# Attention B in 64x64 blocks, with its row maxima added by the mask product

## The reference

```
A_mem  = sigma(q) M / (sigma(q) . z + eps)              sigma(x) = elu(x) + 1
scores = q k^T / sqrt(8), -inf above the diagonal       (64 x 64)
A_dot  = softmax(scores) v
out    = beta A_mem + (1 - beta) A_dot
V_prev = sigma(k) M / (sigma(k) . z + eps)
M      = M + sigma(k)^T (v - V_prev);   z = z + sum(sigma(k))
```

## Time and profile before

| | |
|---|---|
| median of 3 runs | 2139.34 us (2138.98 to 2144.91) |
| the profiled execution's own time | 2121.74 us |
| its span | 2120.0 us |
| mean granted clock of TensorE | 0.854 |
| PE busy | 1713.4 us (81%) |
| DVE busy | 1494.4 us (70%) |
| ACT, POOL busy | 764.9 us (36%), 842.8 us (40%) |
| DMA | 159.66 MB, mean 75 GB/s |

### The profile page before, as it was taken

One profiled execution on the slowest core, in us unless ns is written; L12 is line 12 of the kernel. 1 busy time (PEld: TensorE's weight loads), 2 busy tenths in 40 slices (PEclk: granted clock), 3 DMA queues, 4 the chain that ended last, 5 costly groups with the idle time before them and its releaser, 6 DMA issues. The chain is left out here.

```text
span 2120.0 us, 45990 instructions
## 1 busy us (share of the span) xinstructions
PE 1713.4 (81%) x13668; PEld 1420.0 (67%) x13668; DVE 1494.4 (70%) x3615; ACT 764.9 (36%) x1663; POOL 842.8 (40%) x1054
## 2 busy tenths in 40 slices
PE   5999999999999999947665577787787887787787
PEld 3888888888888888845554355565565665665665
DVE  5678888888888888848885556665666666656655
ACT  1455555555555555522222122222222222222222
POOL 3445544455444455436564423232322232223331
PEclk8999999999999999968886677877887777777868
DMA  3322222222122222123331222222222222212221
GB/s 115 115 93 78 72 72 73 71 71 71 68 73 71 73 73 74 61 66 99 90 97 44 77 66 67 82 75 75 71 72 72 80 75 76 69 66 79 81 70 41
DMA packets 181309, 159.66 MB, mean 75 GB/s; under 512 B 10417, under 2 KB 162609, under 8 KB 181234
## 3 DMA queue, kind: packets, MB, share of 16 engines
q1 hardware_dynamic: 178930, 157.95, 22.6%
q10 hardware_dynamic: 2304, 0.79, 0.2%
HBM read 113.87 MB, written 44.83 MB: 75 GB/s over the span
## 5 line engine op out<-in xcount | busy, mean ns | idle before, releaser
L600 PE MATMUL a_bank<-a_vp,a_prob 128*128 128x96 f32 x4096 | 546.4, 278 | 0.3 <-ACT a_prob L457 0.3
L600 PEld LDWEIGHTS a_bank<-a_vp,a_prob 128*128 128x128 f32 x4096 | 512.8, 197 | 16.8 <-ACT a_prob L457 8.6
L633 DVE TENSOR_REDUCE a_nmax<-a_bank 128x2 f32<-128x512 f32 x512 | 331.7, 686 | 119.2 <-PE a_bank L527 118.8
L457 ACT ACTIVATE a_prob<-a_bank 128x512 f32<-128x512 f32 x512 | 306.0, 598 | 179.3 <-PE a_bank L582 170.5
L1429 ACT ACTIVATE c_prob<-c_bank 128x256 f32<-128x256 f32 x256 | 98.8, 386 | 353.0 <-PE c_bank L1510 317.9
L1707 DVE TENSOR_REDUCE c_nmax<-c_bank 128x4 f32<-128x512 f32 x256 | 168.8, 686 | 69.2 <-PE c_bank L1530 68.7
L527 PE MATMUL a_bank<-a_k_st,a_q_st 96*128 96x256 bf16 x1024 | 208.2, 286 | 7.7 <-DVE a_nmax L633 5.0
L1560 PE MATMUL c_o_bank<-c_vb,c_prob 128*128 128x96 f32 x1024 | 209.1, 339 | 2.3 <-DVE c_ad L1832 1.3
L582 PE MATMUL a_bank<-a_q_st,a_k_st 120*128 120x256 bf16 x1024 | 202.8, 280 | 0.0
L1506 PE MATMUL c_bank<-c_causal_t,c_ident 128*128 128x256 bf16 x256 | 84.9, 332 | 120.6 <-DMA c_q_st<-scratch_c_m_dram 113.8
L1560 PEld LDWEIGHTS c_o_bank<-c_vb,c_prob 128*128 128x128 f32 x1024 | 172.2, 239 | 10.1 <-ACT c_prob L1429 3.0
(11 more groups left out here) (195 smaller groups left out, 3141.6 us busy)
## 6 DMA issues: line engine op xcount, KB each, us to landing
a_q_st<-scratch_a_parts_dram SPq DMA_DIRECT2D x192, 96.0 KB
a_k_st<-scratch_a_parts_dram SPq DMA_DIRECT2D x64, 288.0 KB
c_q_st<-scratch_c_parts_dram SPq DMA_DIRECT2D x192, 96.0 KB
c_k_st<-scratch_c_parts_dram SPq DMA_DIRECT2D x64, 288.0 KB
scratch_a_parts_dram<-a_parts SPq DMA_DIRECT2D x32, 384.0 KB, 2.7
scratch_c_parts_dram<-c_parts SPq DMA_DIRECT2D x32, 384.0 KB, 3.0
a_x<-in_x SPq DMA_DIRECT2D x32, 128.0 KB, 10.7
scratch_y<-a_y SPq DMA_DIRECT2D x32, 128.0 KB, 9.4
```

The costliest lines, as they stand in the source:

```text
L457: act.activation(prob[h % 4][:, :, :].rearrange("p a b -> p (a b)"), t_ps[h % 2][:, :], ACT.Exp).then_inc(exped, 1)
L600: mm = pe.matmul(o_ps[g % 2][:, at:at + VC], prob[h % 4][:, c, t * P:(t + 1) * P], vp[o][:, c, :], start=c == 0, stop=c == NT - 1)
L633: dve.tensor_reduce(nmax[:, t, 2 * g:2 * g + 2], s_ps[t][:, :].rearrange("p (h k) -> p h k", h=2), AX.X, ALU.max, negate=True).then_inc(ma ...
```

## The change

- **First pass.** A unit is now eight heads by two segments: `causal` holds the 64x64 mask eight times, and 16 products of 64 columns each write a 64x64 diagonal block, segment 2t to the lower and segment 2t+1 to the upper 64 partitions. There are four units a batch (NU = 4), one in each of slots 1, 2, 4 and 5, and DVE reduces four times instead of eight.
- **Maxima.** ACT's copy writes the transposed parts into rows 64 to 87 of `late[h2]`, whose rows 0 to 63 hold the causal mask. The second pass's first product has `late` as its moving operand and `pick` as its weights (identity rows for the mask, and for each g rows that pick the three parts of its two heads); it writes mask and maxima at once. The write to DRAM, `shift_rows` and the ones in `k_st` are gone. SP issues `stack(1)` right behind `stack(0)`.
- **Contraction.** Products of both passes contract all 128 rows of the stacks; rows 72 to 127 are zero.
- **Order.** L1541's transposes move behind the transposes of `at` in slot 0, and ACT's `skn` copy to the start of slot 1. On PE, `mem` 0 stands behind slot 1's unit and ahead of the values; `read` 0 ahead of slot 2's unit, `read` 1 behind slot 4's unit, `read` 2 in slot 7. On DVE, `remember` and `read` stand ahead of the slot's reduction, `remember(2)` is interleaved with the second split in slot 6, and `read(2)` is in slot 7.
- **Semaphores.** `stack_in` is now four, one for each buffer and half.

```diff
+        BROWS = SEG + NPART * H // 2
-        causal, causal_t = sb("causal", [P, 512], BF16), sb("causal_t", [P, T], BF16)
+        causal = sb("causal", [P, 512], BF16)
+        pick, late = sb("pick", [BROWS, H // 4, 2, SEG], BF16), two("late", [BROWS, T], BF16)
...
-        mt_ps = ps_a[0:NPART * H // 2, 0:T // 2].bitcast(BF16)
+        mt_ps = ps_a[SEG:BROWS, 0:T // 2].bitcast(BF16)
...
                     stack(0)
-                if active(j, u, 1):
-                    shift_rows(0)
-                    shift_rows(1)
-                if active(j, u, 0):
                     stack(1)
...
-                            act.copy(mt[h2][:, :], mt_ps).then_inc(mt_d, 1)
-                            act.wait_ge(mt_d, 2 * b + h2 + 1)
-                            if h2 or later(j, b, 1):
-                                act.wait_ge(mt_out, (2 * b + h2) * 16)
-                            act.dma_start(m_dram[1 - i, h2], mt[h2][:, :]).then_inc(mt_out, 16)
+                            act.copy(late[h2][SEG:BROWS, :], mt_ps).then_inc(mt_d, 1)
...
                         if g % (ST // 2) == 0:
-                            pe.wait_ge(m_in[g // (ST // 2)], (b + 1) * 16)
+                            pe.wait_ge(mt_d, 2 * b + g // (ST // 2) + 1)
...
-                        pe.matmul(t_ps, ident16[:, :], causal_t[:, :], start=True, stop=True)
+                        pe.matmul(t_ps, pick[:, g % (ST // 2), :, :].rearrange("p a k -> p (a k)"),
+                                  late[g // (ST // 2)][:, :], start=True, stop=True)
...
-                                               k_st[st][0:KROWS, 2 * g + hh, cs], q_st[st][0:KROWS, 2 * g + hh, cs],
+                                               k_st[st][:, 2 * g + hh, cs], q_st[st][:, 2 * g + hh, cs],
...
+                    if s in (2, 7) and active(j, u, 1):
+                        recalled(s // 3)
                     if s in S_AT and active(j, u, 1):
...
+                        pe.matmul(s_ps[t][:, :], ident16[:, :], causal[:, :], start=True, stop=True)
+                        for c in range(H // 2):
+                            for p in range(2):
+                                ts = slice((2 * t + p) * SEG, (2 * t + p + 1) * SEG)
+                                mm = pe.matmul(s_ps[t][p * SEG:(p + 1) * SEG, c * SEG:(c + 1) * SEG],
+                                               q_st[o][:, h2 * H // 2 + c, ts], k_st[o][:, h2 * H // 2 + c, ts],
+                                               start=False, stop=True, skip_group_check=True)
+                        mm.then_inc(score, 1)
+                    if s == 1 and active(j, u, 1):
+                        remembered(0)
+                    if s == 4 and active(j, u, 1):
+                        recalled(1)
...
+                    if s in (3, 5) and active(j, u, 1):
+                        remembered(s // 2)
...
+                    if s == 1 and active(j, u, 1):
+                        for k in range(2):
+                            remember(0, k)
+                    if s == 2 and active(j, u, 1):
+                        for k in range(4):
+                            read(0, k)
+                    if s == 4 and active(j, u, 1):
+                        for k in range(2):
+                            remember(1, k)
+                        for k in range(4):
+                            read(1, k)
                     if s in S_AT and active(j, u, 1):
-                        for t in range(NT):
-                            reduce_unit(S_AT.index(s), t)
+                        reduce_unit(S_AT.index(s))
```

More of the change, by code:

```diff
@@ L1422, in body @@
                 for s in range(ST):
+                    if s == 1 and active(j, u, 1):
+                        b = n - 1
+                        act.wait_ge(sk_p, b + 1)
+                        if later(j, b, 1):
+                            act.wait_ge(mem_p, b * 3)
+                        act.copy(skn[0:SEG, :, :].rearrange("p s f -> p (s f)"),
+                                 ps_c[0:SEG, 0:(NS - 1) * P]).then_inc(sk_d, 1)
                     lag, g = turn(s)
@@ L1494, in body, with remembered, recalled @@
                 o = 1 - i
+                def remembered(c):
+                    b = n - 1
+                    if c == 0:
+                        pe.wait_ge(sk_d, b + 1)
+                        pe.wait_ge(vs_d, 2 * b + 1)
+                    else:
+                        pe.wait_ge(u_d, b * 2 + c)
+                    pe.matmul(ps_c[:, 0:MW], skn[:, c, :], uv[o][:, c, :], start=True, stop=True
+                              ).then_inc(mem_p, 1)
+                def recalled(c):
+                    b = n - 1
+                    pe.wait_ge(mz_d, b * 5 + 2 * c + 1)
+                    pe.matmul(ps_c[:, 0:MW], sg[o][:, c + 1, :, :].rearrange("p a t -> p (a t)"), mz[:, :],
+                              start=True, stop=True).then_inc(read_p, 1)
                 for s in range(ST):
@@ L1534, in body @@
-                    if s == 0 and active(j, u, 1):
-                        b = n - 1
-                        pe.wait_ge(sg_d, b + 1)
-                        if later(j, b, 1):
-                            pe.wait_ge(read_d, b * 9)
-                        apart(pe, spare)
-                        for c in range(NS - 1):
-                            mm = pe.transpose(ps_c[0:SEG, c * P:(c + 1) * P], sg[o][:, c, 0, :], ident[:, :])
-                        mm.then_inc(sk_p, 1)
+                            pe.wait_ge(mask_d, 6)
@@ L1573, in body @@
                         mm.then_inc(at_p, 1)
+                    if s == 0 and active(j, u, 1):
+                        b = n - 1
+                        pe.wait_ge(sg_d, b + 1)
+                        if later(j, b, 1):
+                            pe.wait_ge(read_d, b * 9)
+                        apart(pe, spare)
+                        for c in range(NS - 1):
+                            mm = pe.transpose(ps_c[0:SEG, c * P:(c + 1) * P], sg[o][:, c, 0, :], ident[:, :])
+                        mm.then_inc(sk_p, 1)
                     if s == 5 and active(j, u, 3):
```

137 lines of the change are left out of this document (52 added, 85 removed).

## The result

Faster, but not by as much as forecast: 2044.91 us (median of 4 runs, 2036.56 to 2053.96) against 2139.44 us of the kernel before, a ratio of 0.9553 [0.9496, 0.9611]. The forecast was 1949 us with a range of 1890 to 2010, so the time lies 35 us outside it. The profiled execution took 2052.87 us, with a span of 2050.7.

The account below looks back on a forecast made before the run. Waits and the clock, no full engine, were taken to bound attention B. Per batch 29.0 - 3.8 - 0.5 - 1.3 + 1.6 - 2.1 = 22.9 us, together 190 us saved, giving 1949 us; range 1890 to 2010.

Parts of the forecast that it names:

- maxima in the mask product: Slot 7, second pass: PE's wait for the maxima from DRAM goes, 3.8 us a batch less.
- four units: First pass: four units of 64-column products replace eight units, saving PE 0.5 us a batch.
- other moves of the memory chain: Memory-chain moves other than `read(0)` in slot 2, such as `recalled(2)` and the `sg` transposes: priced at 0.
- the -1.3 for `uv`: Slot 3: `read(0)` ahead of slot 2's reduction on DVE brings `uv` sooner, L1630 1.3 us earlier; bounds 0.7 and 1.7.
- Memory chain in other slots: Moving the memory chain to new slots saves 1.3 us a batch through `read(0)` in slot 2; other moves 0.
- The clock: Low-clock stretches behind the stalls of slots 3 and 7: half regained, 2.1 us a batch; bounds 0 and 4.3.
- 25.0 with none: The batch period in us if none of the lost clock came back, against 22.9 forecast.
- The waits late next: Slot 0: new PE waits for z and `ad`, 0.5 and 1.1 us, together 1.6 a batch; bounds 0.5 and 2.6.
- The unit: First pass: one mask and sixteen 64-column products take 0.77 us at full clock; over 1.2 would refute the forecast.
- rival C: First pass: 64-column products don't stream, 222 ns each; period 35.3 us, time 2328 us; chance 0.03.
- The ring: Path through DRAM from unit 0 to the next unit 0: 21.0 to 23.0 us a batch, nearly binds.
- Rival B: Ring and low clock feed each other through a wait for `stack(0)` before unit 0: 24.8 us, 2007 us; chance 0.22.

Follow-up runs that it names:

- e7: The kernel before with only the maxima added by the mask product (eight units, old slots, 96 rows in the first pass): 1970.86 us.
- e14: The changed kernel with the memory chain in its old slots and 96 instead of 128 contracted rows in both passes: 1949.64 us.
- e6: The changed kernel with the memory chain back in its old slots on PE, DVE and ACT: 1945.92 us.
- after: The changed kernel itself, with every part of the change, against the kernel before: 2044.91 us, ratio 0.9553.
- e13: The changed kernel with only DVE's `remember(1)` moved from slot 4 to the end of slot 3: 1958.88 us.
- e4: The changed kernel with DVE's `normed(1)` moved behind `remember(1)` and `read(1)` in slot 4: 1956.87 us.
- e9: The changed kernel with six unread 512-column products in slot 4 alone, ahead of PE's wait for `mz`: 1969.34 us.
- e11: The changed kernel with the memory chain in its old slots and the stack read by twelve DMAs a half instead of four: 1835.97 us.
- e15: The changed kernel, new slots kept, with the stack read by twelve DMAs a half instead of four: 2041.08 us.
- e1: The changed kernel with ten unread 512-column products a batch put ahead of PE's waits: 1905.22 us.
- e5: The kernel before with unread 512-column products in PE's two stalls, 14 in slot 7 and 6 in slot 3: 2118.35 us.
- e10: The changed kernel with the memory chain in its old slots and unread products in slots 0, 1 and 3 (4, 6 and 3): 1888.20 us.
- e3: The changed kernel with 96 instead of 128 contracted rows in both passes: 2100.32 us.
- e12: The changed kernel with old memory-chain slots, twelve stack DMAs a half, `late` and `pick` padded to 128 rows, and unread products in slots 0 and 3: 1837.52 us.

## Why the prediction was wrong, step by step

The runs cut the period into the prediction's own terms, 29.00 → 24.06 (e7) → 22.87 (e14) → 22.95 (e6) → 26.64 (after):

| step | forecast | measured |
|---|---|---|
| maxima in the mask product, waits for z and `ad`, clock | -3.8 + 1.6 - 2.1 = -4.3 | -4.9 |
| four units, with the wait for `uv` | -0.5 - 1.3 = -1.8 | -1.2 |
| 128 contracted rows | 0 | +0.1 |
| other moves of the memory chain | 0 | **+3.7** |
| sum | -6.1 | -2.4 |

The split holds for this order of the steps. e14 and e6 wait 1.6 and 2.2 us a batch for the stack, so the second and third steps may be worth more than the table gives where the ring is shorter, and the last one costs more. In the prediction the -1.3 for `uv` stood with the memory chain; it is placed here with the units, for the reason given below.

**The step that failed** is "Memory chain in other slots". It followed `read(0)` through slot 2 with care and then said "the other moves I price at 0". Two of them were weighed against the trace, that of `recalled(2)` and that of the `sg` transposes; `remember(1)` was not. On DVE it left slot 3, where its product is ready, and stands behind `normed(1)`, which waits for POOL's `rs`, while on PE `read` 1 moved ahead of the values of slot 4. What is queued behind a waiting instruction was to be named for this pair as well. In its place the runs showed a new wait of PE for `mz`, 1.4 us a batch, and a low clock behind it. e6 undoes the whole step (3.7 us), e13 moves this pair alone (3.3), and e4 leaves the pair and moves `normed(1)` behind it (3.3): both are within 0.01 us of each other. e13 keeps PE's new place, so DVE's place carries the cost; whether PE's old place alone would have covered it wasn't tried.

**The clock** was treated as a bonus with bounds of 0 and 4.3 us. It has another side: the step with a new wait of 1.4 us cost 3.7, of which e9 shows 2.8 to be the clock. Where that wait was missing, the clock rose (0.85 in e7, 0.89 in e6) and the term came in: e7's PE is busy 593.39 us where the kernel before has 676.55 for the same columns, 2.9 us a batch for the 2.1 priced. So the clock term was right for the kernel forecast and wrong for the one that ran; and the bound "25.0 with none" still didn't hold the result, because it kept 1.6 us of waits and had no room for a new one. Why the clock is granted as it is, from which activity, these runs don't settle.

**The -1.3 us for `uv`** came in, but for another reason: e7 has the old slots and keeps the wait, e6 has the old slots and four units and has lost it. So does e14, with 96 rows (4.9 us in 29 batches), which leaves the four units, with one reduction less in the slot; the new place of `read(0)` wasn't needed.

**Right:** the maxima's wait and its 3.8 us, the first part of the change and by itself most of the gain (e7, 1970.86 us). The waits late next: z 0.3 us (7.9/29) and `ad` 1.1 (33.3/29) for 0.5 and 1.1. Reductions, four a batch:

```profile
L1711 DVE TENSOR_REDUCE c_nmax<-c_bank 128x8 f32<-128x512 f32 x116 | 77.8, 679 | 9.4 <-PE c_bank L1533 9.1
```

The unit: the mask's load at 1577.48, sixteen loads in 0.33 us from 1577.91, the values' load at 1578.28, 0.8 us in all against 0.77 (PE, full clock):

```profile
1577.48 0.10 PEld L1529 LDWEIGHTS c_bank<-c_causal,c_ident 128*128 128x128 bf16 x1
1577.91 0.33 PEld L1533 LDWEIGHTS c_bank<-c_k_st,c_q_st 128*64 128x64 bf16 x16 [0.33 <-issue]
1578.28 0.52 PEld L1558 LDWEIGHTS c_o_bank<-c_vb,c_prob 128*128 128x128 f32 x4
```

That is 21 ns a load, so rival C is out. By the rule of the Trainium skill (TensorE: Matmul & The Clock Gate, LDWEIGHTS) a load of 64 columns would take 53 ns, an estimate worked out from its P/1.2 ns; the trace doesn't agree, and the measurement decides. The ring, forecast at 21.0 to 23.0 us, is where e6 stops (22.95, of them 2.2 waiting for the stack), and with the stack read by twelve DMAs the same work takes 19.58 (e11). In `after` it didn't bind (1.5 us of waits in all, and e15). Rival B, the nearest to the result at 2007, had a part of the mechanism, a wait with a low clock behind it, at the wrong wait; that the two feed each other, as B has it, these runs don't show.

**The tail** wasn't in the forecast at all. It is 7.9 us longer, with the clock at 0.53; with fill it is 41.3 us at 0.88 (e1). Which wait begins its low clock wasn't tried.

Of the signs that the prediction named, three showed the failure: PE's largest wait (L1493 instead of the stack's), the clock (0.76 where 0.8 to 0.95 was named) and the traffic (79 GB/s where over 90 was), which follows from the period.

## What to carry to other kernels

When a change reorders instructions, walk through every moved instruction on every engine and ask what now stands ahead of it and what that waits for; an "otherwise 0" must be earned as each priced term is. Price a new wait on TensorE at more than its length, since the clock behind it can cost twice as much again, and price the clock low where a transfer sets the period: 0 in e14 and 0.5% in e5, though 3% in e10, where some of TensorE's work lies on the transfer's own ring. Undo each part alone before judging a change: here the one that looked harmless ate more than half of what the others gave.

## What was not expected of the hardware

- Contracted rows that hold only zeros raise the granted clock: 96 to 128 rows in both passes took it from 0.68 to 0.76 and the time from 2100 to 2045 us (e3), with a product's mean duration nearly the same (L1533 221 and 217 ns); from e14 to e6 the clock went from 0.85 to 0.89, and the time stayed.
- Unread products put into PE's waits took the clock to 1.00 and gave 140 us (e1). Where a transfer bound the stage the same thing gave 0.5% (e5) or 3% (e6 to e10), and where the clock was already 0.99, nothing (e12).
- Four DMAs with an outer repeat of three keep 0.18 to 0.20 of the DMA engines busy, twelve plain ones with the same rows 0.40 to 0.51. SP's issue of a half grew from 2.9 us to 4.1 (3.01 + 1.11) and still 110 us were won (e11).
